# First Mamba layer: another order on TensorE, a bank of its own for the sums, and elementwise steps moved to ScalarE and GpSimd

## The reference

```python
xz = x @ in_proj_w.T
x_p, z = split(xz, 2)                       # 256 channels each
xc = silu(causal_conv(x_p, conv_w, 4 taps) + conv_b)
dt = softplus(xc @ dt_proj_w.T + dt_proj_b)
B_ssm, C_ssm = split(xc @ x_proj_w.T, 2)    # 16 each
s = sum(xc * dt, over channels)
y = sum(s * B_ssm * C_ssm, over the 16) + xc * D_param
y = y * silu(z)
x = x + y @ out_proj_w.T
```

## Time and profile before

| | us |
|---|---|
| three runs | 3399.37, 3394.3, 3399.56 (median 3399.37) |
| profiled execution | 3397.28 |
| its span in the profile | 3395.6 |
| busy: PE, PEld | 2999.0 (88%), 1862.1 (55%) |
| busy: DVE, ACT, POOL | 2418.6 (71%), 1986.3 (58%), 848.6 (25%) |
| mean granted clock of TensorE | 0.952 |
| first Mamba block: first in0, last out | 1283.57, 1490.41 |

### The profile page before, as it was taken

The page is one execution under the profiler, slowest core; times in us unless marked ns, Lnnn a source line. Parts: engine busy times, 40 slices in busy tenths (PEclk is TensorE's granted clock), DMA queues, the critical chain, the costliest instruction groups (busy, mean ns, idle before and its releaser), DMA issues. The chain is left out here.

```text
span 3395.6 us, 44007 instructions
## 1 busy us (share of the span) xinstructions
PE 2999.0 (88%) x14270; PEld 1862.1 (55%) x14270; DVE 2418.6 (71%) x5355; ACT 1986.3 (58%) x3394; POOL 848.6 (25%) x947
## 2 busy tenths in 40 slices
PE   7998889898999997789988788788999998799998
PEld 5766333332777663246554333345577766677776
DVE  5666778784555777778766887867777777577776
ACT  4442667676444445444445666634577776377776
POOL 1020433322000000000002766631133332033332
PEclk8999999998999998889998889899999999799999
DMA  2001112220100330013333222214311110001111
GB/s 88 1 16 32 51 59 67 72 62 31 34 1 1 117 101 7 0 50 99 101 117 104 92 87 80 92 61 131 113 50 34 43 45 9 19 29 51 41 35 53
DMA packets 117869, 193.38 MB, mean 57 GB/s; under 512 B 18396, under 2 KB 31132, under 8 KB 117512
## 3 DMA queue, kind: packets, MB, share of 16 engines
q1 hardware_dynamic: 116056, 187.68, 17.5%
q10 hardware_dynamic: 1584, 2.88, 0.2%
HBM read 172.23 MB, written 18.25 MB: 56 GB/s over the span
## 5 line engine op out<-in xcount | busy, mean ns | idle before, releaser
L420 POOL TENSOR_TENSOR norm_rstd<-norm_rstd,minus_half 128x4 f32<-128x4 f32 (+1 forms) x136 | 176.3, 1296 | 1364.5 <-DVE norm_rstd L407 1354.3
L2510 ACT ACTIVATE main_tiles_r<-banks,feature_cols 128x512 fp32r<-128x512 f32 x512 | 352.8, 689 | 187.7 <-PE banks L262 166.0
L2518 DVE TENSOR_TENSOR main_tiles_r<-main_tiles,main_tiles_r 128x512 fp32r<-128x512 f32 x512 | 382.9, 763 | 68.0 <-ACT main_tiles L2511 66.2
L986 DVE TENSOR_REDUCE gate_scratch<-banks 128x2 f32<-128x1024 f32 (+2 forms) x320 | 344.5, 1112 | 83.4 <-PE banks L251 48.2
L1140 ACT ACTIVATE main_tiles<-banks 128x512 f32<-128x512 f32 (+1 forms) x608 | 316.6, 578 | 137.2 <-PE banks L1121 94.6
L260 PE MATMUL banks<-normed_pairs,moe_weights 128*128 128x512 f32 x740 | 368.4, 498 | 12.9 <-ACT main_tiles L2511 6.5
L2555 POOL TENSOR_TENSOR normed<-normed,main_tiles 128x512 f32<-128x512 f32 x128 | 217.6, 1700 | 532.7 <-DVE main_tiles L2544 532.7
L2511 ACT ACTIVATE main_tiles<-banks,feature_cols 128x512 f32<-128x512 f32 x512 | 349.8, 683 | 0.0
L260 PE MATMUL banks<-main_tiles_r,moe_weights 128*128 128x512 f32 x700 | 308.2, 440 | 31.8 <-DVE main_tiles_r L2518 26.9
L262 PE MATMUL banks<-normed_pairs,moe_weights 128*128 128x512 f32 x740 | 292.1, 395 | 0.0
L261 PE MATMUL banks<-normed_pairs,moe_weights 128*128 128x512 f32 x740 | 291.8, 394 | 0.0
(11 more groups left out here) (376 smaller groups left out, 6686.6 us busy)
## 6 DMA issues: line engine op xcount, KB each, us to landing
main_tiles<-gates_d SPq DMA_DIRECT2D x400, 256.0 KB, 3.3
mamba_tiles<-c_rows_d SPq DMA_DIRECT2D x92, 256.0 KB, 3.3
spare_nat<-c_rows_d SPq DMA_DIRECT2D x36, 256.0 KB, 3.4
found_d<-main_tiles SPq DMA_DIRECT2D x32, 256.0 KB, 2.0
parts_d<-bf_parts SPq DMA_DIRECT2D x48, 128.0 KB, 1.8
q_stacks<-parts_d SPq DMA_DIRECT2D x192, 32.0 KB
k_stacks<-parts_d SPq DMA_DIRECT2D x192, 32.0 KB
weight_staging<-in_w SPq DMA_DIRECT2D x22, 256.0 KB, 3.8
```

The lines of the kernel that those rows point to most:

```text
L420: eng.tensor_tensor(rstd[:, k, 1, 0:w], rstd[:, k, 0, 0:w], minus_half[:, 0:w], ALU.pow).then_inc(s.norm_pow)
L986: eng.tensor_reduce(o.rearrange("p (n s) -> p s n", s=2)[:, :, j0:j0 + per], psum[:, b0:b0 + 2, 0:per * (k1 - k0)].rearrange("p s (n c) -> ...
L2510: eng.activation(pair_3(j)[0], psum[:, 2 + j % 2, :], ACT.Relu, bias=bias)
L2518: eng.tensor_tensor(lo, h3_of(j), hi.bitcast(F32), ALU.subtract).then_inc(s.m3_lo)
```

## The change

Scheduling: MA_US goes from 21.0 to 17.5, nearly all due times of the block change, the next MoE pass is planned from ma_at[-1] + 40.0. Banks: bs moves from bank 2 to bank 7 (for the last chunk to bank 3), bg from bank 3 to bank 2, and bg now comes ahead of bs. Work: the convolution's first product goes to ScalarE as a Copy with a scale (cv0, cv1); m0, m1 go to ScalarE as a Relu; a new part `pool_ma` on GpSimd adds m0 and m1, so that bs is one matmul, and multiplies y by silu(z). Two semaphores are added (ma_sum, ma_y), and num_in of the attention is merged into rec_in. MoE waits that named a moved step name its new owner.

```diff
-                eng.dma_start(num_t, found_d[b, half, :, 0:HD, :]).then_inc(s.num_in, 16)
+                eng.dma_start(num_t, found_d[b, half, :, 0:HD, :]).then_inc(s.rec_in, 16)
...
-            eng.wait_ge(s.num_in, 16 * (k + 1))
-            eng.wait_ge(s.rec_in, 16 * (k + 1))
+            eng.wait_ge(s.rec_in, 32 * (k + 1))
...
+            if n == NC_:
+                eng.wait_ge(*ma_dve(6, "gm"))
...
             if k == 64:
+                eng.wait_ge(*ma_act(7, "g"))
+            if k == 65:
                 eng.wait_ge(*ma_dve(7, "gm"))
-            if k == 65:
-                eng.wait_ge(*ma_act(7, "g"))
...
-    MA_US, MA_LANES = 21.0, 4
+    MA_US, MA_LANES = 17.5, 4
...
-    MA_BANKS = {2: (("in0", 0.0, "dve", "conv0"), ("gate0", 6.8, "act", "sz0"), ("bs", 31.0, "dve", "gm")),
-                3: (("in1", 1.0, "dve", "conv1"), ("gate1", 10.2, "act", "sz1"), ("bg", 35.0, "act", "g")),
-                4: (("dt0", 13.2, "dve", "m0"),), 5: (("dt1", 15.2, "dve", "m1"), ("out", 46.5, "dve", "x")),
-                6: (("bc", 17.5, "dve", "ct"),)}
+    MA_USES = (("in0", 2, 0.0, "dve", "conv0"), ("gate0", 2, 8.5, "act", "sz0"), ("in1", 3, 1.2, "dve", "conv1"),
+               ("gate1", 3, 12.0, "act", "sz1"), ("dt0", 4, 14.0, "act", "m0"), ("dt1", 5, 16.0, "act", "m1"),
+               ("bc", 6, 18.2, "dve", "ct"), ("bg", 2, 31.0, "act", "g"), ("bs", 7, 32.2, "dve", "gm"),
+               ("out", 5, 42.0, "dve", "x"))
+    def ma_bank_of(i, name):
+        return 3 if (i, name) == (NC_ - 1, "bs") else {n: bank for n, bank, _, _, _ in MA_USES}[name]
...  act_ma_front
-                yield ma_at[i] + 1.9 + 1.1 * blk
+                yield ma_at[i] + 1.8 + 1.4 * blk
...
+                if i >= MA_LANES:
+                    eng.wait_ge(*ma_pe(i - MA_LANES, "out"))
+                eng.activation(ma_tile(i, f"xc{blk}"), psum[:, 2 + blk, :], ACT.Copy,
+                               scale=col("m1conv", 6 + blk)).then_inc(ma_act(i, f"cv{blk}")[0])
...
-                yield ma_at[i] + 6.6 + 3.4 * blk
+                yield ma_at[i] + 7.0 + 3.8 * blk
...
-                yield ma_at[i] + 8.8 + 3.4 * blk
+                yield ma_at[i] + 10.0 + 3.4 * blk
...  dve_ma_conv
-                yield ma_at[i] + 2.6 + 3.4 * blk
-                eng.wait_ge(*ma_act(i, f"tail{blk}"))
-                if i >= MA_LANES:
-                    eng.wait_ge(*ma_pe(i - MA_LANES, "out"))
+                yield ma_at[i] + 3.2 + 3.2 * blk
+                eng.wait_ge(*ma_act(i, f"cv{blk}"))
...
-                eng.tensor_scalar(t, v, col("m1conv", 6 + blk), None, ALU.mult).then_inc(s.ma_conv)
...  pe_ma_back
-            eng.wait_ge(*ma_dve(i, "dt1"))
-            eng.matmul(psum[:, 2, :], ones[:, :], ma_tile(i, "m0"), start=True, stop=False)
-            eng.matmul(psum[:, 2, :], ones[:, :], ma_tile(i, "m1"), start=False, stop=True).then_inc(ma_pe(i, "bs")[0])
...
+            eng.wait_ge(s.ma_sum, i + 1)
+            eng.matmul(psum[:, ma_bank_of(i, "bs"), :], ones[:, :], ma_tile(i, "m0"), start=True,
+                       stop=True).then_inc(ma_pe(i, "bs")[0])
...
-            eng.wait_ge(*ma_dve(i, "y1"))
+            eng.wait_ge(s.ma_y, 2 * i + 2)
...  act_ma_back: due times 16.0, 18.2 (abs), 20.5, 21.3 (exp), 29.0 (bt), 37.2 (g) become
+                yield ma_at[i] + 16.4 + 2.0 * o
+                eng.wait_ge(*ma_pe(i, f"dt{o}"))
+                eng.activation(a, psum[:, 4 + o, :], ACT.Abs, bias=col("m1dtb", o)).then_inc(ma_act(i, f"abs{o}")[0])
+                if o == 0 and i >= MA_LANES:
+                    eng.wait_ge(*ma_pe(i - MA_LANES, "bs"))
+                eng.activation(ma_tile(i, f"m{o}"), psum[:, 4 + o, :], ACT.Relu,
+                               bias=col("m1dtb", o)).then_inc(ma_act(i, f"m{o}")[0])
+                yield ma_at[i] + 20.8 + 0.7 * o
...
+            yield ma_at[i] + 28.0
...
+            yield ma_at[i] + 33.0
...  dve_ma_back
-                yield ma_at[i] + 17.5 + 2.3 * o
-                eng.wait_ge(*ma_act(i, f"abs{o}"))
-                eng.tensor_scalar(m[o], psum[:, 4 + o, :], col("m1dtb", o), 0.0, ALU.add, ALU.max).then_inc(ma_dve(i, f"m{o}")[0])
-                yield ma_at[i] + 25.5 + 1.8 * o
+                yield ma_at[i] + 25.2 + 1.7 * o
...
-                yield ma_at[i] + 26.4 + 1.8 * o
+                yield ma_at[i] + 26.1 + 1.7 * o
...
-            yield ma_at[i] + 31.5
+            yield ma_at[i] + 29.5
...
-            yield ma_at[i] + 39.0
+            yield ma_at[i] + 35.2
...
-                yield ma_at[i] + 40.3 + 2.2 * k
+                yield ma_at[i] + 36.5 + 1.2 * k
...
-                yield ma_at[i] + 41.4 + 2.2 * k
-                eng.wait_ge(*ma_dve(i, f"y{k}a"))
-                eng.tensor_tensor(xc[k], xc[k], sz[k], ALU.mult).then_inc(ma_dve(i, f"y{k}")[0])
-            yield ma_at[i] + 49.5
+            yield ma_at[i] + 45.0
...
+    def pool_ma(eng, chunks):
+        for i in chunks:
+            yield ma_at[i] + 29.8
+            m0, m1 = ma_tile(i, "m0"), ma_tile(i, "m1")
+            eng.wait_ge(*ma_dve(i, "dt1"))
+            eng.tensor_tensor(m0, m0, m1, ALU.add).then_inc(s.ma_sum)
+            for k in range(2):
+                xc, sz = ma_tile(i, f"xc{k}"), ma_tile(i, f"sz{k}")
+                yield ma_at[i] + 38.2 + 1.5 * k
+                eng.wait_ge(*ma_dve(i, f"y{k}a"))
+                eng.tensor_tensor(xc, xc, sz, ALU.mult).then_inc(s.ma_y)
...
-    plan_moe1(ma_at[-1] + 44.0)
+    plan_moe1(ma_at[-1] + 40.0)
```

More of the change, by code:

```diff
@@ L71 @@
 ring_pe ring_free at_top shift_out shift_in0 shift_in1 shift_in2
-at_score at_exp at_tri at_pv at_acc found_out0 found_out1 den_in den_rec rec_out rec_in num_in num_rec
+at_score at_exp at_tri at_pv at_acc found_out0 found_out1 den_in den_rec rec_out rec_in num_rec
 nat_in neg_ready
@@ L1670, in pe_m1_second @@
             if k == 64:
-                eng.wait_ge(*ma_dve(7, "m0"))
+                eng.wait_ge(*ma_act(7, "m0"))
             if k == 65:
@@ L1726, in numbered @@
         return {name: n + 1 for n, name in enumerate(names.split())}
-    MA_PE = numbered("in0 in1 gate0 gate1 dt0 dt1 bc bs bg out")
-    MA_ACT = numbered("tail0 tail1 silu0 sz0 silu1 sz1 abs0 abs1 exp0 exp1 ln0 ln1 bt g")
-    MA_DVE = numbered("conv0 conv1 m0 m1 m0a dt0 m1a dt1 ct gm y0a y0 y1a y1 x")
+    MA_PE = numbered("in0 in1 gate0 gate1 dt0 dt1 bc bg bs out")
+    MA_ACT = numbered("tail0 cv0 tail1 cv1 silu0 sz0 silu1 sz1 abs0 m0 abs1 m1 exp0 exp1 ln0 ln1 bt g")
+    MA_DVE = numbered("conv0 conv1 m0a dt0 m1a dt1 ct gm y0a y1a x")
     def ma_pe(i, name):
@@ L1768, in pe_ma_front @@
             for name in ("in0", "in1", "gate0", "gate1"):
-                bank, after = MA_STEP[name]
-                yield ma_at[i] + after
+                bank = ma_bank_of(i, name)
+                yield ma_at[i] + MA_AT[name]
                 if name == "in0":
@@ L1798, in dve_ma_conv @@
         for i in chunks:
-            count = 6 * i
+            count = 4 * i
             c = ACROSS[i]
@@ L1845, in pe_ma_back @@
             z.then_inc(ma_pe(i, "bc")[0])
-            yield ma_at[i] + MA_STEP["bs"][1]
-            eng.wait_ge(*ma_bank_free(i, "bs"))
-            eng.wait_ge(*ma_dve(i, "dt1"))
-            eng.matmul(psum[:, 2, :], ones[:, :], ma_tile(i, "m0"), start=True, stop=False)
-            eng.matmul(psum[:, 2, :], ones[:, :], ma_tile(i, "m1"), start=False, stop=True).then_inc(ma_pe(i, "bs")[0])
-            yield ma_at[i] + MA_STEP["bg"][1]
+            yield ma_at[i] + MA_AT["bg"]
             eng.wait_ge(*ma_bank_free(i, "bg"))
             eng.wait_ge(*ma_dve(i, "ct"))
-            eng.matmul(psum[:, 3, :], ones[0:16, :], ma_tile(i, "a1")[0:16, :], start=True, stop=True).then_inc(ma_pe(i, "bg")[0])
-            yield ma_at[i] + MA_STEP["out"][1]
+            eng.matmul(psum[:, 2, :], ones[0:16, :], ma_tile(i, "a1")[0:16, :], start=True, stop=True).then_inc(ma_pe(i, "bg")[0])
+            yield ma_at[i] + MA_AT["bs"]
+            eng.wait_ge(*ma_bank_free(i, "bs"))
+            eng.wait_ge(s.ma_sum, i + 1)
+            eng.matmul(psum[:, ma_bank_of(i, "bs"), :], ones[:, :], ma_tile(i, "m0"), start=True,
+                       stop=True).then_inc(ma_pe(i, "bs")[0])
+            yield ma_at[i] + MA_AT["out"]
             eng.wait_ge(*ma_bank_free(i, "out"))
-            eng.wait_ge(*ma_dve(i, "y1"))
+            eng.wait_ge(s.ma_y, 2 * i + 2)
             for k, x in enumerate((xc0, xc1)):
@@ L1865, in act_ma_back @@
             a0, a1 = ma_tile(i, "a0"), ma_tile(i, "a1")
-            yield ma_at[i] + 16.0
-            eng.wait_ge(*ma_pe(i, "dt0"))
-            eng.activation(a0, psum[:, 4, :], ACT.Abs, bias=col("m1dtb", 0)).then_inc(ma_act(i, "abs0")[0])
-            yield ma_at[i] + 18.2
-            eng.wait_ge(*ma_pe(i, "dt1"))
-            eng.activation(a1, psum[:, 5, :], ACT.Abs, bias=col("m1dtb", 1)).then_inc(ma_act(i, "abs1")[0])
-            for o, a in enumerate((a0, a1)):
-                yield ma_at[i] + 20.5 + 0.8 * o
```

(7 more changed lines are left out.)

31 lines of the change are left out of this document (15 added, 16 removed).

## The result

The kernel after takes **3385.95 us** (median of 17 runs, 3378.35 to 3392.12) against 3396.24 (17 runs, 3391.89 to 3400.91) for the kernel before: a ratio of 0.997, 95% interval 0.9961 to 0.9978. That is 10.3 us or 0.3% less, inside the range and 3 us above the forecast time. The gain forecast was 16.3 us; of the 6 us between the two gains 3.1 are the kernel before, whose median was 3399.37 in the three runs that the forecast started from.

A forecast was written before the change was run, and what follows sets the result against it. The first Mamba was taken as bound by a chain through all engines, none full. Frames 1 to 6 give 12.8 us and the tail 3.5, together 16.3 off: median 3383 us, range 3370 to 3393.

The forecast's parts named there:

- The walk of the new order: First Mamba, one chunk's in0 to the next's, followed engine by engine with prices: 21.5 us against 23.6.
- (b): L1895, two per chunk, becomes a ScalarE Relu (0.68 us); VectorE's wait for L1868 goes, breaking the old ring.
- the old ring: First Mamba before: chain through all engines in fixed orders; TensorE waits 35.3 us for L1902, VectorE 35.2 for L1868.
- (c): The y products (2 x 0.65 us) go from VectorE to GpSimd at 1.27 each; hidden, slack 1.5 us.
- (d): m0 + m1 on GpSimd, 1.27 us, saves one of the two matmuls of bs; hidden beside ct and bg.
- (a): Convolutions' first products to ScalarE: 1.56 us off VectorE, conv1 ends before ln0 either way, cv1's 0.69 on the path.
- (e): bs in bank 7, free of the gates: price nothing in the frames, some tenths in the tail.
- (f): num_in folded into rec_in and swapped waits for k = 64, 65: same last event waited for, 0.
- A: Rival: clock doesn't fall in the new order; frame 20.1, 27 us off, 3372; chance 0.19 including what lies between.
- B: Rival: slow clock to end of bs, or cv, extra waits and norm back cost 1 us; frame 22.7, 3391; chance 0.18.
- D: Rival: slower, half speed lasts to the end of dt1; frame 26.0, deciding from 23.6; 3412; chance 0.05.
- C: Rival: nothing to gain, bc and cv eat what the ring gave; frame 23.6, 3399 within 3; chance 0.06.

The follow-up runs named there:

- the second profile: The kernel after run again with no edit, for another profile: 3384.26 us, ratio 0.9959 to the kernel before.
- the kernel with the four matmuls: Kernel after plus four matmuls per chunk, result unread, in TensorE's idle time ahead of the norm's transposes: 3377.95 us, ratio 0.9949 to the kernel before.
- bc later alone: Kernel after with bc(i-1) issued behind in1(i) on TensorE, nothing else changed: 3382.19 us, ratio 0.9961 to the kernel before.
- every hole filled: Kernel after with bc behind in1, five unread matmuls per chunk and eight in the tail: 3360.23 us, ratio 0.9891 to the kernel before.

## Why the prediction came out right, step by step

**The walk of the new order held.** In the short frame shown, the ln was waited for until 9.1 us after in0 (walked 9.2) and ct ended at 14.3 (walked 14.3). VectorE's timeline of the two:

```profile
1345.87 0.69 DVE L1905 TENSOR_TENSOR mamba_tiles<-mamba_tiles 128x512 f32<-128x512 f32 x1 [1.02 <-ACT mamba_tiles L1889]
...
1350.39 0.68 DVE L1911 TENSOR_TENSOR mamba_tiles<-banks,mamba_tiles 16x512 f32<-16x512 f32 x1
```

TensorE's hole is 4.96 us where 5.0 was walked, and it stands where it was put. The norm's transposes begin at 11.9, as walked, and bg at 14.6.

**The clock behind the hole is the step that was right only as a mean.** I let the half speed last 5.25 us, from the nearest row of before, and got 21.5 us for every frame. No frame has that length: it is 20.3 or 23.8, four against two in one execution and two against four in the other. The sums are 128.8 and 136.1, so that the first agrees with the forecast 129.0 by luck, and the second has 7 us more. The working has a slip too: a bg of 1.05 us is 2.1 at half speed, which from 14.65 leads to 16.75 and not 16.5, and carried on the frame is 21.8. The six frames would have been better written as so many short ones and so many long ones. The Trainium skill ("TensorE: Matmul & The Clock Gate", "Part 1: The HAM clock gate") has the clock set by how busy TensorE has been recently. The same section calls the number of slow matmuls at a start variable from run to run. The traces agree with both: half speed stands behind every hole of 4.96 us, and behind it, at restarts within the kernel, how long it lasts differs between frames with equal orders and equal holes.

**(b), "the wait of VectorE for L1868 is gone, which breaks the old ring", failed as a cause.** The walk used both edits and so had the right sum, but the sentence gives the credit to one. The Relu alone moved nothing (0.9999), as VectorE then waits for g; the order without the moved work made it slower (1.0029), with ct 2.1 us later. What is shown is that both halves are needed. Of the moved work two shares are known from the full-speed frames, 0.9 us a frame for the sum and 0.6 in odd chunks for the first product; the Relu's own share in the new order stays open.

**(c) and (d) were right, (a) by half.** By (a) conv1 ends ahead of ln0 either way, so that moving the convolution's first product would only put cv1's 0.69 us on the path. It costs 0.1 in even chunks and is worth 0.6 in odd ones, where by the walk's own prices conv1 without the move ends at 9.8, behind ln0 at 9.2. The y products are hidden in the frames. The sum on GpSimd is never waited for and saves the 0.9 us that one matmul less should. (e) and (f) were not run singly.

**GpSimd against VectorE: nothing in the frame, as said, but the tail has it.** In the frames the pair of y products lasts 2.96 us where one takes 1.27:

```profile
1336.85 2.96 POOL L1937 TENSOR_TENSOR mamba_tiles<-mamba_tiles 128x512 f32<-128x512 f32 x2 [5.44 <-DVE mamba_tiles L1920]
```

It agrees with the rule weighed in the prediction (the Trainium skill, "SBUF — State Buffer", "Who interferes with whom"), by which y0 waits for y1a: the pair takes 0.4 us more than twice 1.27, where the prediction had 0.7, off the path and inside the slack. The sum beside ct (1350.44 to 1351.70 in the frame shown) takes 1.26 us, as one that meets nothing.

**The tail failed: 3.5 us less was forecast, 2.0 more came** (56.8 against 54.8; 56.9 in the second profile). The step that failed is "gm is some 1 to 2.6 sooner": gm of the last chunk starts 42.8 us after in0, before it was 40.2, so 2.6 later. The first fence is the kernel after, the second the kernel before:

```profile
1441.68 3.78 PE L1844 MATMUL banks<-mamba_tiles,mamba_weights 128*128 128x512 f32 x4
...
1463.70 2.07 PE L1857 MATMUL banks<-mamba_tiles,ones 16*128 16x512 f32 x2
1465.70 2.08 PE L1861 MATMUL banks<-mamba_tiles,ones 128*128 128x512 f32 x2
...
1467.88 0.69 DVE L1916 TENSOR_TENSOR mamba_tiles<-banks,mamba_tiles 128x512 f32<-128x512 f32 x1 [2.57 <-PE banks L1861]
```

```profile
1476.29 2.05 PE L1849 MATMUL banks<-mamba_tiles,ones 128*128 128x512 f32 x2 [2.34 <-DVE mamba_tiles L1902]
...
1481.08 1.12 PE L1854 MATMUL banks<-mamba_tiles,ones 16*128 16x512 f32 x2
...
1482.87 0.69 DVE L1910 TENSOR_TENSOR mamba_tiles<-banks,mamba_tiles 128x512 f32<-128x512 f32 x1 [0.17 <-ACT mamba_tiles L1886]
```

Before, bs ran ahead of the routing's transpose and bg alone behind it, at full speed. In the new order both stand behind it, bs last, and both at half speed; gm waits 2.57 us for bs, and the scaling of the next norm (L433) stands behind gm on VectorE. That norm's transposes come 44.8 us after in0, before 42.6, which is the whole loss. Ahead of that, dt0 of the last chunk ran at half speed (3.78 us), so that dt1 started at 22.6 instead of 20.2 and ln0, forecast 0.8 us sooner, was later by 1.2.

Something else is in the tail that I had not looked for. There the routing of the first MoE chunk runs on VectorE, in instructions of 0.19 us each (0.19 for this form before as well), and some of them fall beside a product on GpSimd. GpSimd's timeline and VectorE's, kernel after:

```profile
1451.42 1.27 POOL L1937 TENSOR_TENSOR mamba_tiles<-mamba_tiles 128x512 f32<-128x512 f32 x1 [11.23 <-DVE mamba_tiles L1920]
1453.47 1.27 POOL L1937 TENSOR_TENSOR mamba_tiles<-mamba_tiles 128x512 f32<-128x512 f32 x1 [0.79 <-DVE mamba_tiles L1920]
1460.15 1.26 POOL L1932 TENSOR_TENSOR mamba_tiles<-mamba_tiles 128x512 f32<-128x512 f32 x1 [5.41 <-DVE mamba_tiles L1908]
```

```profile
1451.69 1.04 DVE L1449 TENSOR_TENSOR gate_scratch<-gate_scratch 128x32 f32<-128x32 f32 x1
1453.74 1.05 DVE L1459 TENSOR_TENSOR gate_scratch<-gate_scratch 128x32 f32<-128x32 f32 x1
1460.20 1.26 DVE L1479 TENSOR_TENSOR gate_scratch<-gate_scratch 128x32 f32<-128x32 f32 x1
```

Each of these three begins during a GpSimd product and ends with it, 0.9 to 1.1 us late. That this is GpSimd's doing the next two kernels show. With the y products on VectorE (first fence) the first two instructions are short and the third is not; with the sum on TensorE (second fence) it is the other way round:

```profile
1454.81 0.19 DVE L1449 TENSOR_TENSOR gate_scratch<-gate_scratch 128x32 f32<-128x32 f32 x1
1456.73 0.19 DVE L1459 TENSOR_TENSOR gate_scratch<-gate_scratch 128x32 f32<-128x32 f32 x1
...
1462.47 1.26 DVE L1479 TENSOR_TENSOR gate_scratch<-gate_scratch 128x32 f32<-128x32 f32 x1
```

```profile
1447.89 1.04 DVE L1449 TENSOR_TENSOR gate_scratch<-gate_scratch 128x32 f32<-128x32 f32 x1
...
1456.40 0.19 DVE L1479 TENSOR_TENSOR gate_scratch<-gate_scratch 128x32 f32<-128x32 f32 x1
```

What it costs the tail is less than the three delays. From the routing's first matmul to its transpose (L1392) it is 13.0 us in the kernel with the four matmuls, 12.9 with the y products on VectorE and 12.0 with the sum on TensorE: only the third delay is on the path. There the tail stays as long (53.9 against 54.1), since the sum's second matmul stands behind the transpose and from the norm's transposes to the first bias it is 1.0 us more, at a mean clock of 0.61 instead of 0.69. Without the y's on GpSimd the tail was longer (56.7 against 54.1): 1.6 us of it are there by the routing's first matmul, since the half speed, which began with dt0 in the other kernel, was there in bg already and went on through bs, and 0.8 come from the y products that stand ahead of L489 on VectorE. That out(6) waits 2.68 us for GpSimd's y is off the path, as TensorE then stands idle for another 3.79 us for VectorE.

With bc later alone the tail was 53.7 us at clock 0.78, with every hole filled beside it 48.1 at 0.93.

**Rivals.** A (20.1 a frame) is in the result as the short frames. The long ones are what B and D name, the half speed lasting to the end of bs: B priced it at 22.7 a frame and D put its dividing point at 23.6 (26.0 if dt1 ran cold too); measured are 23.8, with dt1 at full speed. B's other reason isn't there, the chain is as long as walked. The mean frame of the second profile is 22.7, B's own figure, and the median lies 3 us from the forecast and 5 from B's, so that the runs hardly tell the two apart. C (3399, within 3) is excluded by the ratio, 0.9961 to 0.9978.

**The signs.** Borne out: L1895's wait gone, TensorE's idle time of 5 us ahead of the norm's transposes, half speed behind it, bs of two passes, GpSimd 5.2 us busy a frame, three table loads. Not borne out: no frame of 21.5, and VectorE's main wait is for bs (36.9 us) and not for the ln (6.0). And of what the prediction called wrong, two things are there: in0 to in0 is over 23 us in two frames of six (four in the second profile), and out waits for GpSimd once, in the tail. The time came out near because long and short frames, a tail 5.5 us worse than forecast, and stretches outside the block sum to it.

## What to carry to other kernels

Where an engine stands idle some microseconds per period, price the restart as two cases per period, short and long, and count periods; then try to fill the hole with work that nobody reads: with that and two changed places in the order (bc and the norm), the gain here grew from 10 us to 43. Undo a change of order and of placement separately before crediting either: in a ring of in-order queues one half can be worth nothing and the other a loss. Work moved to GpSimd is free only where VectorE's instructions beside it are off the path: here an instruction of 0.19 us took up to 1.26 beside one of GpSimd's. At the end of a block walk the order again, with what follows the block in it: bs behind bg costs nothing that shows in the frames, and in the tail gm waited 2.57 us for it.

## What was not expected of the hardware

- The same program behind the same hole of 4.96 us ran dt0 in 1.82 us at clock 1.00 or in 3.57 at 0.50, in frames next to each other, and the number of each differed between executions (two of six long, then four of six).
- Behind a hole of only 1.08 us dt0 took 3.33 us in one frame and 1.98 in another, which had more idle time ahead of it.
- A VectorE instruction of 128x32 with both inputs in SBUF took 1.04 to 1.26 us beside a GpSimd product of 128x512, against 0.19 alone.
